# Four-layer attention and feed-forward kernel on one core: attention scores in float32 row bands, output bias on GpSimd, layer 3's correlation loops in 64x64 tiles

## The chip, the core and the metric

The kernel is one program on one core of a Trainium2 chip. The metric is device time in microseconds of that core, lower is better. Engines: PE (TensorE, matmuls; its weight loads are listed as PEld), DVE (VectorE), ACT (ScalarE), POOL (GpSimd) and SP (SyncE, which here only issues DMAs). Each engine works through its own list in order and waits on semaphores that others raise.

## The reference

`x` is 2 batches x 1024 rows x 256 features; `ctx` has 154 rows per batch. Four layers follow each other, each `x = x + attention(layernorm(x), ctx)` and then `x = x + ffn(layernorm(x))`. In layers 0 to 2 the attention has 16 heads of 16 features:

```python
q, k, v = split(x_n @ Wq + bq), split(ctx @ Wk + bk), split(ctx @ Wv + bv)
# layer 2 has no biases, and turns q and k by rotary angles
out = softmax(q @ k.T / 4) @ v
x = x + out.reshape(...) @ Wo + bo
```

Layer 3's attention is an autocorrelation: a circular correlation of q and k over 1024 positions, its mean over a head's features, the 6 best shifts and their softmax, the sum of v rolled by these shifts with these weights, and an output projection. The feed-forward parts: layer 0 squares a ReLU between two ternary weight matrices with a low-rank addition; layer 1 adds a dense gated part and, for each row, 32 rows of an expert table chosen by top-8 in 4 heads; layer 2 has 8 experts (2 chosen) and 2 shared ones; layer 3 has 8 experts (2 chosen). All is float32.

## The kernel before

**Chunks and order.** `x` stays in SBUF as `x_sb`, 16 tiles of 128 rows; a chunk `c` is 4 tiles (512 rows). The attention of a chunk of layers 0 to 2 is called here (layer, c). The twelve run in the order `A_ORDER`: (0,0) (0,1) (1,0) (1,1) (0,2) (0,3) (1,2) (1,3) (2,0) (2,1) (2,2) (2,3). `plan()` writes down every item of these layers with an assumed duration and what it waits for, ranks items by the longest path behind them, and from that fixes once, ahead of the run, the order of the list of every engine. Attention uses PSUM banks 0 to 3, the normalised rows, projections and keys banks 4 and 5, the feed-forward parts banks 6 and 7. Layer 3 is a fixed sequence whose phases begin with `enter` and end with `leave`: a phase starts when the other engines have ended theirs.

**Scores before.** Float32 values are split in three bfloat16 parts. Queries: PE projects (L686), ACT writes a float32 and a bfloat16 copy (L1099, L1100; in layer 2 DVE applies the rotary turn, L1337 to L1341), DVE subtracts and rounds to the other parts (`split`, L1325 to L1327), SP writes the parts to DRAM (L1779) and reads them back in 7 DMAs (L1788) so that the 7 pairs of parts of one head stand in 112 partitions. The keys go the same way (L1801, L1811). There is one buffer of queries, so the read of a chunk waits for the last score of the chunk before.

**One attention chunk.** The first pass (`p1`): 12 units, each of 6 (or 4) heads of one row tile, PE L726, then DVE takes the maximum over the 154 keys (L1385; L1388 and L1389 for the units of 4). PE turns the maxima (L734), ACT copies them (L1114), a DMA puts them as row 112 beside the queries (L1794). The second pass (`s`): for each head one bfloat16 matmul of 113x128x512 (L744) in banks 0 and 1 by turns and one exponential on ACT (L1121); for each group of four heads the last 26 keys (L752, L1128); then the weighting with v (`w`): L763 over the rest keys of four heads, and four matmuls of 32 columns each (L766), one per head, each with its own moving operand and its own 32 partitions of bank 3; ACT copies (L1132). Then transposes and division (L776, L1397, L1398, L783), and the output projection, where a one-row matmul adds the bias in layers 0 and 1 (L793, L796), and DVE adds to `x_sb` (L1322).

**The expert rows of layer 1.** For each row tile 32 table rows are fetched in 8 groups of 4. GpSimd issues 4 indirect DMAs per group (L1691) into a ring of 4 groups; DVE multiplies (L1261), ACT sums (L1048), DVE and ACT weigh (L1268, L1269, L1057), DVE adds three rows (L1278 to L1280), GpSimd the fourth (L1702, L1705). A group's slot is free when these adds are done.

**Layer 3.** `corr(b)`: per batch `b` and half `g` of the features, for two blocks `N` of 512 positions 10 accumulating matmuls of 128x128x512 (L969). Their stationary operand `kst` holds 8 heads' keys as diagonal blocks of 16x16, all else is zero. ACT copies the result to `c1` (L1219, L1220), SP writes it to DRAM (L1842) and reads it skewed (L1847), `top(b)` sums over features on PE (L958), and picks shifts and weights on DVE (L1575 to L1592); SP writes the weights to DRAM (L1830) and reads them shifted for every row (L1834). `out3(b)` is the second loop of the same size (L981, stationary `vst`, also diagonal blocks), ACT copies (L1228), the output projection (L992) and the add to `x_sb`. The sequence on PE is corr(0), projection of chunks 2 and 3, top(0), corr(1), first half of out3(0), top(1), second half, projection, the layer norm of chunk 0, out3(1). On DVE top(1) stands ahead of the adds of out3(0).

Of the kernel before, what the change touches and what calls it, by code (L numbers as in the profile page):

```python
# [10 lines left out]
P = 128  # L11
B, T, D = 2, 1024, 256
S = 154
# [5 lines left out]
SP_ = 160  # L19
# [17 lines left out]
Q_PARTS, K_PARTS = (0, 0, 0, 1, 1, 1, 2), (0, 1, 2, 0, 1, 2, 0)  # L37
NB = len(Q_PARTS)
MROW = NB * DH
SWAP = [lane ^ 1 for lane in range(32)]  # L40
MAX_UNITS = [(i, h, min(h + 6, H)) for i in range(TI) for h in range(0, H, 6)]
# [7 lines left out]
FFN3_PACK = dict(gate=KT * E3, we=KT * E3 * D, be=D)  # L49
CONST_PACK = dict(ident=P, mask8=8, padrow=1, iota8=8, selh=2 * 32, valid=SP_)  # L50
# [22 lines left out]
def plan():  # L73
# [26 lines left out]
    def kv(layer, b):  # L100
        item = (layer, b)
        shared.append(("kv",) + item)
        old = (layer - 1, 2 * b + 1) if layer else None
        k1 = add("PE", ("kv",) + item, 5.0, ld["kv", layer], ("SP", ("in", "ctx")), ("SP", ("in", "const")), banks[0])
        k2 = add("ACT", ("kv",) + item, 0.9, k1, parts[0])
        k3 = add("DVE", ("kv",) + item, 8.0 if layer == 2 else 5.5, k2, old and ("PE", ("w",) + old + (G4 - 1,)),
                 ld["rope", 0 if b == 0 else 2] if layer == 2 else None)
        banks[0] = k3
        parts[0] = add("SP", ("kvW",) + item, 0.1, k3, land=4.0)
        return add("SP", ("kvR",) + item, 0.7, parts[0], old and ("PE", ("r",) + old + (G4 - 1,)), land=5.0)  # L110
# [23 lines left out]
    def queries(layer, c, xt, k):  # L134
        item = (layer, c)
        shared.append(("Q",) + item)
        q1 = add("PE", ("Q",) + item, 3.3, xt, ld["q", PIECE_AT[k]])
        use["xta"] = q1
        if layer < 2:
            q2 = add("ACT", ("Q",) + item, 2.8, q1, parts[0], use["xa"])  # L140
            q3 = add("DVE", ("Q",) + item, 3.2, q2)
            banks[0] = q2
        else:
            q3 = add("DVE", ("Q",) + item, 9.0, q1, parts[0], use["xa"], ld["rope", c])
            banks[0] = q3
        use["xa"] = q3
        before = A_ORDER[k - 1] if k else None
        parts[0] = add("SP", ("QW",) + item, 0.1, q3, before and ("SP", ("L",) + before), land=3.8)
        return add("SP", ("L",) + item, 0.7, parts[0], before and ("PE", ("r",) + before + (G4 - 1,)), land=10.0)

    def attention(layer, c, k, keys_in, queries_in):
# [7 lines left out]
        for u in range(NU):  # L159
            p = pe("p1", 0.65, *((on("PE", "p1", u - 1), u > 1 and on("DVE", "p1", u - 2)) if u else  # L160
                                 (queries_in, keys_in, before and ("DVE", ("y",) + before + (TI - 1,)))), n=(u,))
            top = add("DVE", ("p1", layer, c, u), 1.15, p)
        p = pe("mt", 0.6, top)
        a = add("ACT", ("mt", layer, c), 0.6, p)
        last = add("SP", ("mt", layer, c), 0.1, a, land=2.3)
        for G in range(G4):
            for j in range(4):
                h = 4 * G + j
                z = (G, j - 2) if j >= 2 else (G - 1, j + 2)
                last = pe("s", 0.38, last, z[0] >= 0 and on("ACT", "s", *z), n=(G, j))  # L170
                add("ACT", ("s", layer, c, G, j), 0.62, last, h >= 6 and on("PE", "w", (h - 6) // 4),
                    on("ACT", "s", G, j - 1) if j else G and on("ACT", "r", G - 1))
            last = pe("r", 0.6, last, G and on("ACT", "r", G - 1), n=(G,))
            a = add("ACT", ("r", layer, c, G), 0.72, last, on("ACT", "s", G, 3), G >= 2 and on("PE", "w", G - 2))
            w = pe("w", 2.2, a, G and on("ACT", "w", G - 1), n=(G,))
            add("ACT", ("w", layer, c, G), 0.62, w)
        for G in range(G4):
# [1786 lines left out]
```

## Time and profile before

| | us |
|---|---|
| median of 3 runs | 2049.45 (2047.57 to 2050.88) |
| the profiled execution | 2054.53 |
| its span | 2052.7 |
| busy: PE / DVE / ACT / POOL | 1449.3 / 1186.3 / 805.8 / 659.3 |

The span is the time from the first to the last instruction of the profiled execution. Matmuls are pipelined, so a busy PE is not PE at its peak. The granted clock of PE over the span was 0.816 of full speed. Busy shares are means over stages that differ: the gathers of expert rows run from 395 to 1429 us only.

### The profile page before, as it was taken

Reading aid. Unit: us, or ns where it says so; the run is one execution under the profiler, and the core shown is the slowest. Engines: PE = TensorE matmul, PEld = TensorE weight load, DVE = VectorE, ACT = ScalarE, POOL = GpSimd, SP = SyncE. Lnnn points to the kernel's source line nnn. Section 1 sums busy time; section 2 is a strip of 40 time slices with the busy share of each in tenths; the row PEclk is TensorE's granted clock in tenths of the full one; section 3 lists DMA queues with packets and bytes.
Section 4 is the critical chain, followed back from the end, with each engine's and each line's share of the span. In section 5 each row is a group of like instructions: output and inputs, shape, how many; then the busy total and the mean of one; then the engine's idle time right before and its main releaser. Section 6 shows DMA issues by size and latency. Waiting matters only on the chain.

```text
span 2052.7 us, 17985 instructions
## 1 busy us (share of the span) xinstructions
PE 1449.3 (71%) x5190; PEld 752.3 (37%) x5190; DVE 1186.3 (58%) x3091; ACT 805.8 (39%) x2135; POOL 659.3 (32%) x672
## 2 busy tenths in 40 slices
PE   4788686876864865544365467567788668998998
PEld 2344343432432433222223333333444334344444
DVE  7342426588765856877578677776533223331665
ACT  2334143456563665344363548437343012101210
POOL 0000000235576676757565576674000000011000
PEclk7799798877775876766678688778899999999999
DMA  8331431537459567555655756853300011210000
GB/s 230 63 37 16 59 47 26 86 94 163 125 160 211 146 194 176 151 139 166 154 146 163 161 159 174 191 157 99 57 1 8 0 43 25 57 53 15 11 11 21
DMA packets 106513, 205.04 MB, mean 100 GB/s; under 512 B 32624, under 2 KB 68080, under 8 KB 105776
## 3 DMA queue, kind: packets, MB, share of 16 engines
q0 software_dynamic: 40960, 134.25, 24.2%
q1 hardware_dynamic: 65456, 69.66, 16.5%
q8 instruction: 41, 0.67, 0.1%
q14 instruction: 56, 0.46, 0.1%
HBM read 187.94 MB, written 15.73 MB: 99 GB/s over the span
## 4 chain that ended last, share of the span: by engine, by line
PE 40%; DVE 18%; POOL 13%; DMA 11%; issue 9%; ACT 7%; SPq 1%; ACTq 0%; DVEq 0%; POOLq 0%
POOL bufR L1691 11%; DMA bufB<-scr_queries 6%; PE psum L1012 6%; PE psum L905 5%; DMA bufR<-in_table,rowid 4%; PE psum L981 3%; PE psum L969 3%; PE psum L915 2%; DVE m L1385 2%; POOL half_sum L1705 2%; PE psum L835 2%; PE psum L871 2%; PE psum L843 1%; PE psum L793 1%; PE psum L726 1%
## 5 line engine op out<-in xcount | busy, mean ns | idle before, releaser
L1691 POOL DMA_INDIRECT bufR<-in_table,rowid x512 | 542.6, 1060 | 647.7 <-DVE prob L1498 391.2
L1048 ACT ACTIVATE bufR<-bufR 128x256 f32<-128x256 f32 x512 | 205.6, 406 | 222.3 <-DVE bufR L1261 213.2
L1261 DVE TENSOR_TENSOR bufR<-bufR 128x1024 f32<-128x1024 f32 x128 | 161.4, 1261 | 146.9 <-DMA bufR<-in_table,rowid 146.3
L905 PE MATMUL psum<-xtf,wf 128*128 128x512 f32 x320 | 165.1, 664 | 45.7 <-DVE x_sb L1545 34.2
L726 PE MATMUL psum<-bufB 112*128 112x154 bf16 x768 | 92.8, 276 | 142.4 <-DMA bufB<-scr_queries 77.2
L1713 POOL TENSOR_TENSOR x_sb<-x_sb,wattn 128x256 f32<-128x256 f32 x16 | 11.0, 722 | 418.3 <-ACTq L509 376.9
L1385 DVE TENSOR_REDUCE m<-psum 128x6 f32<-128x924 f32 x96 | 105.8, 1116 | 66.1 <-PE psum L726 63.2
L726 PEld LDWEIGHTS psum<-bufB 112*128 112x128 bf16 x768 | 70.1, 118 | 189.4 <-issue 104.5
L744 PE MATMUL psum<-bufB 113*128 113x512 bf16 x192 | 76.1, 432 | 79.5 <-ACT bufR L1121 62.2
L1322 DVE TENSOR_TENSOR x_sb<-x_sb,psum 128x256 f32<-128x256 f32 x128 | 50.8, 417 | 139.3 <-PE psum L992 50.0
L915 PE MATMUL psum<-wf,bufR 128*128 128x256 f32 x320 | 93.8, 447 | 50.9 <-DVE bufR L1536 42.5
L1121 ACT ACTIVATE bufR<-psum 128x512 f32<-128x512 f32 x192 | 109.4, 596 | 45.3 <-PE psum L744 45.1
L1705 POOL TENSOR_TENSOR half_sum<-half_sum,bufR 128x256 f32<-128x256 f32 x112 | 92.4, 825 | 105.6 <-ACT bufR L1057 102.7
L1012 PE MATMUL psum<-wf,xtf 128*128 128x512 f32 x256 | 121.1, 632 | 0.5 <-DVE x_sb L1655 0.5
L905 PEld LDWEIGHTS psum<-xtf,wf 128*128 128x128 f32 x320 | 64.9, 212 | 129.2 <-issue 71.6
L871 PE MATMUL psum<-xtf,wf 128*128 128x512 f32 x128 | 80.4, 786 | 36.9 <-DVE bufR L1456 36.9
L1048 ACT ACTIVATION_READ_ACCUMULATOR bufR<-bufR 128x1 f32 x512 | 97.3, 190 | 0.0
L915 PEld LDWEIGHTS psum<-wf,bufR 128*128 128x128 f32 x320 | 67.9, 221 | 76.9 <-issue 66.5
L1057 ACT ACTIVATE bufR<-bufR,ew 128x256 f32<-128x256 f32 x128 | 63.8, 500 | 62.6 <-DVE ew L1269 61.3
L763 PE MATMUL psum<-bufR,bufB 128*128 128x512 f32 x96 | 66.8, 784 | 27.5 <-ACT bufR L1128 26.2
L1545 DVE SCALAR_TENSOR_TENSOR x_sb<-psum,bufR,x_sb 128x256 f32<-128x256 f32 x128 | 53.1, 478 | 52.0 <-PE psum L915 51.5
L1536 DVE TENSOR_TENSOR bufR<-bufR,psum 128x512 f32<-128x512 f32 x40 | 27.4, 685 | 96.3 <-ACT bufR L1176 96.0
(236 smaller groups left out, 2693.6 us busy)
## 6 DMA issues: line engine op xcount, KB each, us to landing
bufB<-scr_queries SPq DMA_DIRECT2D x84, 256.0 KB
scr_queries<-bufB SPq DMA_DIRECT2D x12, 768.0 KB
bufR<-in_table,rowid POOLq DMA_INDIRECT x512
wf<-in_ffn SPq DMA_DIRECT2D x2, 2304.0 KB, 14.5
bufB<-scr_keys SPq DMA_DIRECT2D x42, 80.0 KB
bufR<-in_ffn SPq DMA_DIRECT2D x1, 2696.5 KB, 16.3
wattn<-in_attn SPq DMA_DIRECT2D x4, 641.0 KB
bufR<-scr_roll SPq DMA_DIRECT2D x4, 592.0 KB
```

The costliest lines, as they stand in the source:

```text
L726: ins = mm(psum[:, pair + z, at:at + S], queries[0:MROW, h, i * P:(i + 1) * P], keys(b)[0:MROW, h, 0:S], start=True, stop=True)
L744: mm(bank(j % 2), keys(b)[0:MROW + 1, 4 * G + j, 0:P], queries[0:MROW + 1, 4 * G + j, :], start=True, stop=True).then_inc(at_s2, 1)
L871: ins = mm(bank(6 + r), w1(name)[:, kt, m * P:(m + 1) * P], xtf[:, kt, :], start=kt == 0, stop=kt == KT - 1)
L905: ins = mm(bank(6 + r), gu[:, kt, r, :], xtf[:, kt, :], start=kt == 0, stop=kt == KT - 1)
L915: ins = mm(psum[:, 6 + i // 2, i % 2 * D:(i % 2 + 1) * D], hm2[:, GUS.index(m) % 7, i * P:(i + 1) * P], down2[:, m, :], start=m == ms[0], ...
L1012: ins = mm(bank(y % 4), xtf[:, kt, i * P:(i + 1) * P], w3("we")[:, kt, e * 512:(e + 1) * 512], start=kt == 0, stop=kt == KT - 1)
L1048: own.mark(act(row, row, ACT.Identity, accum_out=dots[:, g % 4, j:j + 1]))
L1121: act(probs[h % 6], bank(j % 2), ACT.Exp).then_inc(at_ex, 1)
L1261: tt(rows, rows, cast(xg[c % 3][:, i, :].unsqueeze(1), [P, GRP, D]), ALU.mult).then_inc(f1_mu, 1)
L1385: eng.reduce_max(m4[:, i, h0:h1].rearrange("p (a b) -> p a b", a=2), psum[:, pair:pair + 2, 0:3 * S].rearrange("p a (b s) -> p a b s", b=3 ...
L1691: eng.indirect_dma_start(ring[:, s * GRP + j, :], None, io["table"], bass.IndirectOffsetOnAxis(ap=rowid[c % 3][:, at + j:at + j + 1], axis ...
L1705: eng.tensor_tensor(half_sum[:, :], half_sum[:, :], up, ALU.add).then_inc(f1_half, 1)
```

## The change

- **Scores.** Queries and keys stay float32 in SBUF, nothing is split or goes through DRAM, and the maxima stay in SBUF. A band of 32 partitions holds two heads; `keysm[..., par, :]` is the keys with the other head of each pair set to zero. A first-pass unit is two float32 matmuls of 32x128x308 in two bands (four heads), 16 units per chunk. A second-pass burst is four float32 matmuls of 32x128x512, one per band, into banks 0 to 3, and four bfloat16 matmuls with a constant `sel` that subtract the maxima; then ACT takes two exponentials of 1024 columns. A burst starts when ACT has done with the one before. Per chunk there are 4 such bursts and 2 for the rest keys. There are two buffers of queries.
- **Keys and values.** The rest keys of v come from one full matmul with a repeated context `ctx4`; the v bias is added by DVE.
- **Output bias.** GpSimd adds it to `x_sb` (4 adds per chunk, layers 0 and 1), after the chunk's layer norm has read it; its list is shared with the gathers.
- **Layer 3.** Both loops run as 64x64 tiles, with the blocks that are zero left out: per `u` four matmuls of 64x64x512. The results lie in another layout, so 6 DMAs write each `c1`, and ACT copies in `out3(b)` come after each half. `Wo` comes with layer 3's feed-forward weights.
- `plan()` has new durations and no DMA items of the scores; all lists come out in a new order.

```diff
-Q_PARTS, K_PARTS = (0, 0, 0, 1, 1, 1, 2), (0, 1, 2, 0, 1, 2, 0)
+BANDS, PAR = 4, 2
-MAX_UNITS = [(i, h, min(h + 6, H)) for i in range(TI) for h in range(0, H, 6)]
+MAX_UNITS = [(i, g, half) for i in range(TI) for g in range(2) for half in range(2)]
...
             def first_pass(layer, c, u):
-                for h in range(h0, h1):
-                    z, at = (h - h0) // 3, (h - h0) % 3 * S
-                    ins = mm(psum[:, pair + z, at:at + S], queries[0:MROW, h, i * P:(i + 1) * P], keys(b)[0:MROW, h, 0:S],
+                for z in range(2):
+                    r = band(2 * side + z)
+                    ins = mm(psum[:, 2 * (u % 2) + z, 0:PAR * S], q[r, g, i * P:(i + 1) * P], keysm[r, g, b, :, 0:S],
                              start=True, stop=True)
...
-            def score(layer, c, G, j):
+            def score(layer, c, g, par):
...
+                elif par:
+                    eng.wait_ge(at_ex, 12 * k + 6 * g + 2)
+                else:
+                    eng.wait_ge(at_ex, 12 * k + 6)
+                    eng.wait_ge(at_ou, 4 * k + 2)
+                for z in range(BANDS):
+                    mm(bank(z), keysm[band(z), g, b, par, 0:P], q[band(z), g, :], start=True, stop=False)
+                for z in range(BANDS):
+                    ins = mm(bank(z), sel[band(z), 2 * g + par, :], mt[band(z), :], start=False, stop=True)
+                ins.then_inc(at_s2, 1)
...
             def corr(b):
                 for g in range(2):
-                    for N in range(2):
-                        for u in range(U):
-                            ins = mm(bank(2 * g + N), kst(b, g)[:, u, :], qx[:, g, 16 * u + N * 512:16 * u + N * 512 + 512],
-                                     start=u == 0, stop=u == U - 1)
+                    for u in range(U):
+                        for N in range(2):
+                            for r in range(2):
+                                h = half(r)
+                                ins = mm(psum[half(N), 2 * g + r, :], kst(b, g)[h, u, h], qx[h, g, 16 * u + N * 512:16 * u + N * 512 + 512],
+                                         start=u == 0, stop=u == U - 1, skip_group_check=True)
                     ins.then_inc(co_c, 1)
...
             def project_out(layer, c, i):
-                if layer < 2:
-                    ins = mm(psum[:, at, 0:D], valid[:, 0:P], wattn[0:1, AC["bo"]], start=False, stop=True)
...
+                for side in range(2):
+                    act(probs[side][:, par:4:2, :], psum[:, 2 * side:2 * side + 2, :], ACT.Exp).then_inc(at_ex, 1)
...
-                split(qf, [qparts[:, z] for z in range(3)]).then_inc(sk_p, 1)
...
+                for par in range(PAR):
+                    ts(keysm[:, :, b, par, :], kts, parity[:, par:par + 1], None, ALU.mult)
+                    ins = ts(keyr[:, :, b, 32 * par:32 * par + 32], kts[:, :, P:SP_], parity[:, par:par + 1], None, ALU.mult)
...
+            def add_bias(layer, c):
+                eng.wait_ge(ld_o, 16 * (PIECE_AT[chunk(layer, c)] + 1))
+                eng.wait_ge(fr_xn, TI * (front_of["a", layer, c] + 1))
+                for i in range(TI):
+                    ins = eng.tensor_tensor(x_sb[:, c * TI + i, :], x_sb[:, c * TI + i, :], wattn[:, AC["bo"]], ALU.add)
+                ins.then_inc(at_bo, 1)
...
-            def load_queries(layer, c):
-                for z in range(NB):
-                    eng.dma_start(queries[z * DH:(z + 1) * DH], scrq[Q_PARTS[z]].rearrange("(h d) n -> d h n", d=DH))\
-                        .then_inc(sk_rd, 16)
-            def turn_max(layer, c):
-                eng.dma_start(queries[MROW:MROW + 1], mt[:, :]).then_inc(at_mr, 16)
...
-                    eng.dma_start(scr1[a], c1[g]).then_inc(co_wr, 16)
+                    for r in range(2):
+                        for N in range(2):
+                            eng.dma_start(scr1[a, half(r), N * 512:(N + 1) * 512], c1[g][half(N), r * 512:(r + 1) * 512])\
+                                .then_inc(co_wr, 16)
+                        eng.dma_start(scr1[a, half(r), T:T + 16], c1[g][half(0), r * 512:r * 512 + 16]).then_inc(co_wr, 16)
```

`out3(b)` changes as `corr(b)` does, with `vst` and `roll` in place of `kst` and `qx`.

## Rows read from the trace of the kernel before

**Rows 1.** The page, part 2: PE clock granted, in 40 slices.
```profile
PEclk7799798877775876766678688778899999999999
```
**Rows 2.** Windows by stage: length, busy per engine (instructions), PE clock, DMA share, GB/s.
```profile
0.00:395.00 395.00, 286.11 (x1284) 152.87 (x1284) 183.62 (x498) 138.58 (x240) 2.97 (x17) 0.83 0.36 66
395.00:1429.00 1034.00, 639.09 (x2320) 335.61 (x2324) 754.72 (x1911) 535.25 (x1678) 645.31 (x640) 0.74 0.61 157
1429.00:1687.00 258.00, 188.07 (x694) 102.89 (x687) 95.93 (x265) 76.91 (x113) 0.00 (x0) 0.93 0.09 16
1687.00:2052.00 365.00, 336.05 (x896) 160.90 (x896) 152.07 (x420) 55.03 (x104) 10.98 (x16) 0.95 0.11 33
```
**Rows 3.** Chain that ended last: shares by line, then pieces: start, us, what.
```profile
POOL bufR L1691 11%; DMA bufB<-scr_queries 6%; PE psum L1012 6%; PE psum L905 5%; DMA bufR<-in_table,rowid 4%; PE psum L981 3%; PE psum L969 3%; PE psum L915 2%; DVE m L1385 2%; POOL half_sum L1705 2%; PE psum L835 2%; PE psum L871 2%; PE psum L843 1%; PE psum L793 1%; PE psum L726 1%
...
107.96 15.41 DMA bufB<-scr_queries
...
1466.34 14.10 DMA bufB<-scr_queries
```
**Rows 4.** Waits from 395 to 1429: who <- whom: us, times, longest.
```profile
POOL bufR L1691 <- issue: 133.1, 398, 2.0
POOL half_sum L1705 <- ACT bufR L1057: 102.7, 21, 18.7
...
PE psum L726 <- DMA bufB<-scr_queries: 55.9, 5, 19.9
POOL bufR L1691 <- DVE x_sb L1280: 55.4, 25, 9.4
```
**Rows 5.** Groups of instructions: shapes, count | busy us, mean ns of one | idle before.
```profile
L1121 ACT ACTIVATE bufR<-psum 128x512 f32<-128x512 f32 x192 | 109.4, 596 | 45.3 <-PE psum L744 45.1
L1385 DVE TENSOR_REDUCE m<-psum 128x6 f32<-128x924 f32 x96 | 105.8, 1116 | 66.1 <-PE psum L726 63.2 <-issue 1.1
L796 PE MATMUL psum<-wattn,const 1*128 1x256 f32 x64 | 32.2, 595 | 0.0
L1388 DVE TENSOR_REDUCE m<-psum 128x3 f32<-128x462 f32 x48 | 30.3, 632 | 8.5 <-PE psum L726 7.8 <-issue 0.8
L1325 DVE TENSOR_TENSOR xa<-xa,bufB 128x1024 f32<-128x1024 f32 x12 | 15.3, 1271 | 26.2 <-ACT bufB L1100 26.0
L1713 POOL TENSOR_TENSOR x_sb<-x_sb,wattn 128x256 f32<-128x256 f32 x16 | 11.0, 722 | 418.3 <-ACTq L509 376.9 <-DVEq L509 41.4
L1219 ACT ACTIVATE bufR<-psum 128x1024 f32<-128x1024 f32 x4 | 4.1, 1023 | 60.3 <-PE psum L969 60.3
```
**Rows 6.** Timeline of PE, weighting and FFN 1: start, us, line, rows*columns, count.
```profile
91.48 2.05 PE L763 MATMUL psum<-bufR,bufB 128*128 128x512 f32 x2
93.46 1.94 PE L766 MATMUL psum<-bufR,bufB 128*32 128x512 f32 x8
...
342.07 1.13 PE L863 MATMUL psum<-wf,bufR 64*128 64x256 f32 x8 [2.33 <-DVE bufR L1461]
```
**Rows 7.** Timeline of layer 3's loops and the selection.
```profile
1713.95 34.60 PE L969 MATMUL psum<-bufR,bufB 128*128 128x512 f32 x80
...
1763.58 3.62 PE L958 MATMUL psum<-bufR,const 128*32 128x512 f32 x8 [1.46 <-ACTq L509]
...
1767.34 1.21 DVE L1575 COPY bufR<-psum 16x1024 f32<-16x1024 f32 x1 [16.34 <-PE psum L958]
...
1784.81 0.80 SPq L1830 DMA_DIRECT2D scr_roll<-bufR  x2
...
1843.20 1.23 SPq L1834 DMA_DIRECT2D bufR<-scr_roll  x2
...
1849.83 1.40 DVE L1304 BATCH_NORM_STATS2 stats<-x_sb 128x6 f32<-128x256 f32 x4
...
1858.79 35.12 PE L981 MATMUL psum<-bufR,bufB 128*128 128x512 f32 x80
```
**Rows 8.** Windows after the second read of the weights: columns as in Rows 2.
```profile
1853.00:1858.00 5.00, 0.94 (x5) 0.97 (x6) 1.66 (x3) 2.07 (x4) 2.39 (x4) 0.52 0.00 0
```

More of the change, by code:

```diff
@@ L136, in queries @@
         shared.append(("Q",) + item)
-        q1 = add("PE", ("Q",) + item, 3.3, xt, ld["q", PIECE_AT[k]])
+        q1 = add("PE", ("Q",) + item, 3.6, xt, ld["q", PIECE_AT[k]])
         use["xta"] = q1
+        old = k >= 2 and ("PE", ("r",) + A_ORDER[k - 2] + (1,))
         if layer < 2:
-            q2 = add("ACT", ("Q",) + item, 2.8, q1, parts[0], use["xa"])
-            q3 = add("DVE", ("Q",) + item, 3.2, q2)
-            banks[0] = q2
-        else:
[L144 to L149, printed above, removed]
+            banks[0] = add("ACT", ("Q",) + item, 1.3, q1, old)
+        else:
+            banks[0] = add("DVE", ("Q",) + item, 5.0, q1, old, ld["rope", c])
+        return banks[0]
     def attention(layer, c, k, keys_in, queries_in):
@@ L182, in attention @@
             a = add("ACT", ("o", layer, c, g), 0.62, p)
+        if layer < 2:
+            bias = add("POOL", ("bo", layer, c), 3.0, ("ACT", ("N4", "a", layer, c)), ld["o", PIECE_AT[k]])
+        else:
+            bias = None
         for i in range(TI):
-            p = pe("y", 1.2, a, ld["o", PIECE_AT[k]], i and on("PE", "y", i - 1), n=(i,))
-            out = add("DVE", ("y", layer, c, i), 0.43, p)
+            p = pe("y", 0.9, a, ld["o", PIECE_AT[k]], i and on("PE", "y", i - 1), n=(i,))
+            out = add("DVE", ("y", layer, c, i), 0.43, p, bias)
         return out
@@ L714, in first_pass @@
                 k, b = chunk(layer, c), c // 2
-                i, h0, h1 = MAX_UNITS[u]
-                pair = 2 * (u % 2)
+                i, g, side = MAX_UNITS[u]
+                q = queries[:, k % 2]
                 if u == 0:
@@ new lines, in score, with score_rest @@
+                for z in range(BANDS):
[3 more added lines that the diff above has]
+                ins.then_inc(at_s2, 1)
+            def score_rest(layer, c, g):
+                k, b = chunk(layer, c), c // 2
+                q = queries[:, k % 2]
+                eng.wait_ge(at_ex, 12 * k + 6 * g + 4)
+                for side in range(2):
+                    for z in range(2):
+                        r = band(2 * side + z)
+                        mm(psum[half(z), side, :], keyr[r, g, b, :], q[r, g, :], start=True, stop=False, skip_group_check=True)
+                for side in range(2):
+                    for z in range(2):
+                        r = band(2 * side + z)
+                        ins = mm(psum[half(z), side, :], selr[r, g, :], mt[r, :], start=False, stop=True, skip_group_check=True)
@@ L1363, in kv @@
                     own.wait()
-                    own.link(tt(kts, kts, ksw, ALU.add))
-                own.link(eng.tensor_copy(kparts[:, 0], kts))
-                split(kts, [kparts[:, z] for z in range(3)]).then_inc(kv_p, 1)
+                    own.link(tt(kts[:, :, 0:S], kts[:, :, 0:S], ksw[:, :, 0:S], ALU.add))
+                if layer:
+                    eng.wait_ge(at_s2, 6 * (chunk(layer - 1, 2 * b + 1) + 1))
+                for par in range(PAR):
+                    ts(keysm[:, :, b, par, :], kts, parity[:, par:par + 1], None, ALU.mult)
+                    ins = ts(keyr[:, :, b, 32 * par:32 * par + 32], kts[:, :, P:SP_], parity[:, par:par + 1], None, ALU.mult)
+                ins.then_inc(kv_p, 1)
                 eng.wait_ge(kv_v, j + 1)
```

377 lines of the change are left out of this document (166 added, 211 removed).

## The prediction

> **What bounds the kernel now.** I read the windows by stage first. They cut the span at the first gather (395 us) and after the last (1429), at the end of layer 2 (1687) and at the end [rows 2]. No engine is full in the first three: PE is busy for 72%, 62% and 73% of them, DVE for 73% of the second. Only in the last is PE 92% busy. So the first three are held by handoffs, and the chain of waits says by which. The gather instructions on GpSimd are 11% of it, the read of the split queries 6%, which is 121 us in seven pieces of about 14 to 20 us, the first at 107.96 and the last at 1466.34 [rows 3]. The other five chunks have their read beside other work. In the middle stage GpSimd is the closest to full: 645 us busy and 133 us in issue, 778 of 1034 [rows 2, 4]. Its other idle time is in waits for ACT (103) and DVE (55), that is, for ring slots not yet given back [rows 4]. Five times PE stands on the read of queries, 55.9 us in all [rows 4], and as every list is fixed, DVE and ACT then stand on PE. In layer 3 the two loops are the chain: 34.60 us per batch and loop [rows 7].
>
> **Do tiles of the array run side by side?** Everything that follows hangs on this, and the trace shows two of the three kinds. Four matmuls of 32 columns (8 pieces: a float32 matmul is two) take 1.94 us; one full matmul (2 pieces) takes 2.05 beside it [rows 6]. So four column tiles cost one. Four matmuls of 64 rows and 256 columns, 8 pieces, take 1.13 us [rows 6]; a piece of 512 takes 34.60/80 = 0.43 at the high clock [rows 7], so 8 pieces of 256 in a row would take 1.73, in pairs 0.86 plus the pipeline's end. So row tiles pair too. Bands of 32 rows and 64x64 tiles are in no row. Bounds: one matmul's time for a burst of four, or four. I take the first, as both neighbours do.
>
> The Trainium skill, "TensorE: Matmul & The Clock Gate", Part 3, gives 3.07x, not 4x, for four row tiles of K=32 and N=512. Estimated from that page, each of the 72 bursts would cost 0.3 of 0.86 to 1.7 us more, 19 to 37 us of PE, and the sum below would be about 1905. The column tiles above show no such loss. "TensorEngine Tiling (Array Packing)", Tiling Modes, speaks against the change as well: a change of mode drains the array. From L763's start to L766's are 1.98 us where two pieces at the low clock are 1.72 [rows 6, 7], which agrees with at most 0.26 per change; some 10 more changes a chunk would be 31 us of PE, beside waits for the most part.
>
> **Layer 3, from 1713.95.** Each loop of a batch is 20 groups of four tiles, 2 pieces each: 20 x 2 x 0.43 = 17.3 for 34.6, four times. What is late next is the selection between the loops. By rows, with corr(0) starting at 0:
> - corr(0) ends at 17.3 (before 34.6). To top(0) it was 15.0 (1748.55 to 1763.58) [rows 7], with copy, write and skewed read in it; twelve DMAs per batch in place of two, on SP ahead of the read, add 1: top(0) at 33.3, corr(1) at 36.9, its end at 54.2.
> - DVE's selection: copy at 1767.34, weights handed to SP at 1784.81, 17.5 [rows 7]. Then write and shifted read: the second read starts at 1843.20 [rows 7] and the DMA engines are idle from 1853 on [rows 8], so about 10, and 2.5 for the write before it. Ready at 36.9 + 17.5 + 12.5 = 67. So out3(0) starts at 67 and not at 55: PE stands for 12 us that corr(1) used to cover, and starts again at the low clock (+2).
> - Half of out3(0), 8.6, top(1) 3.6 [rows 7], half: 90. But top(1) ends at 81, DVE is in its selection until 98.5, and the adds of out3(0) stand behind it in DVE's list. PE does two of the four projections and waits. Adds done at 104. Before, they were done at 1849.83, that is 135.9.
> - Layer norm to out3(1) as before, 1849.83 to 1858.79: 113 (before 144.8). The second read is ready at 98.5 + 12.5 = 111, just hidden.
> - out3(1) saves 17.4, and loses 0.6 as both copies come after its end.
>
> Sum: 32 + 17 = 49 of the 69 that the loops lose; I take 48. Bounds: 38 (reads slower by 5 each, all low clock) and 55.
>
> **Start to the first gather, 395 us.** Out: three reads on the chain, about 15.6 each (the first is at 107.96 [rows 3]), 47 us. Also the head: the first unit of chunk (0,0) can follow the query projection and doesn't wait for DRAM; the ternary weights then compete for DVE, so I take 13 (bounds 0 and 30). In: the bursts. Before, exponentials (596 ns each [rows 5]) ran beside matmuls. Now a burst is 1.07 us of PE at the high clock or 2.1 at the low (2 pieces of float32, 1 bfloat16 pass taken as half a piece of 0.43), then ACT 2 x 1.02 [rows 5] with PE idle, four times, and twice a shorter one: some 17 to 24 us per chunk beside nothing of its own, where the 12.5 us of exponentials had the weighting (4 x 4.0 at the low clock [rows 6]) beside them. Alone that is 8 to 16 per chunk; feed-forward work fills part, I take 5: +20 for four chunks. First-pass: a unit on DVE of 616 columns lies between 632 (462) and 1116 ns (924) [rows 5], 0.79; 16 units are 12.7, as before (8 x 1.12 + 4 x 0.94). PE's side of a unit is 0.52 at the high clock but 1.03 at the low: +4 there, inside the 5. The one-row bias matmuls, 32 us of PE in eight chunks, go [rows 5]. Sum -47 - 13 + 20 = -40; bounds -75 and +10.
>
> **The gathers, 1034 us.** GpSimd's floor is 778 + 4 bias items of 4 x 0.72 [rows 5] = 790, so at most 244 can go. What goes for certain: DVE's split, three instructions like L1325 (1.27, the cast less) [rows 5], 3.4 us x 7 chunks = 24 out of a list that the ring waits for. Of PE's 55.9 on reads I count 36, as the ring covers the rest. The bias items put 12 us in GpSimd's list, half of it in time that it has: +6. Bursts hold ACT no longer than before (8 x 1.02 against 16 x 0.60). Sum -54. Bounds: 0, if the ring sets the pace by itself, and -150, if what is held is the attention chain, which loses reads in each of seven chunks.
>
> **After the gathers to layer 3, 258 us.** Out: the read of (2,3), 14.1 [rows 3], and its write. The bursts of (2,3) lie beside layer 2's experts, and layer 2's own loop of one matmul, ACT, DVE, matmul is not touched. I take 12 more for (2,2) being further on at the last gather: -30; bounds 0 and -65.
>
> **The sum.** 2054.5 - 40 - 54 - 30 - 48 = 1882.5 against the profiled execution, which is 0.25% above the median; forecast 1878.
>
> **Rivals.**
> - *The ring sets its own pace.* For it: 778 of 1034 us, and 398 short waits called issue [rows 4]; against: 158 us of waits for ACT and DVE. The middle gains nothing: 1932.
> - *The attention chain held the middle.* For it: chunks whose reads stand open on PE; against: DVE 73% busy. The middle gives 130 and not 54: 1802.
> - *Bursts starve PE (slower).* Place: ACT's list from 395 to 1429. A chunk has 10 handoffs between PE and ACT with nothing in flight; each may queue behind ACT's sums of a gather group, and PE falls to the low clock, which it has already for half of this stage (0.74 [rows 2]; dips in [rows 1]). Price: half of ACT's share of a burst in queueing, 1.0, and 1.0 for PE's share at the low clock in place of the high (2.1 and 1.07), is 2.0 on 12 x 10 handoffs, 240, of which 20 are in the forecast: 2098. It decides from 1.6 per handoff on (1878 - 20 + 192 = 2050). Against: fewer handoffs, filled by other items.
> - *Bands and 64x64 tiles run one after another (slower), so the change doesn't do what it says.* A group of four tiles takes 3.43 in place of 1.72 for two full matmuls, 80 groups, +137 in place of -48; each of 72 bursts 2.6 more, each first pass 16 x 0.52, +287: 1878 + 48 + 137 + 287 = 2350. Against: [rows 6].
>
> **Chances.** Forecast 0.52 (its own range 1840 to 1915), ring 0.22, attention chain 0.16, starving 0.06, serial 0.04. A measurement of this kernel can tell 0.2% (4 us) from no change. Faster 0.89, same 0.02, slower 0.09. The range 1790 to 1965 leaves out the two slower rivals and the far end of the chain rival.
>
> **What would show it.** L1788, L1779 and L1325 are gone, and no chunk's first unit waits for a DMA. The loops of layer 3 take 17 to 18 us per batch each, with an idle of 10 to 14 ahead of out3(0) that ends on a DMA, and DVE's adds of out3(0) wait for PE no more but stand behind the selection. The first gather is at about 355, gather groups take about 7.6 us (now 8.1), and the last tile's add is at about 1335. A burst's four float32 matmuls start together. Wrong would be: loops of over 25 us, a middle stage longer than 1034, or PE's clock under 0.65 in it.

## The result, and the profile after

The changed kernel takes 1916.15 us (median of 4, 1904.04 to 1918.98) against 2050.16 for the kernel before in the same runs (2047.57 to 2061.31): ratio 0.9325, 95% interval 0.9272 to 0.9379. On another chip it took 1922.93 (median of 5), ratio 0.9350 (0.9327 to 0.9373), and experiments are read against both. The forecast was 1878 in a range of 1790 to 1965: faster, as forecast, but 38 us short of it and 1 us outside the forecast's own range. The profiled executions span 2052.7 before and 1916.5 after, 136 less, and all stages gained.

The windows by stage of the changed kernel, cut at the same events as [rows 2] (first gather, last tile's add, end of layer 2). Columns: stretch, length, then busy PE, PEld, DVE, ACT, POOL with their instructions, PE clock, DMA share, GB/s.

```profile
0.00:381.10 381.10, 312.58 (x1338) 155.26 (x1338) 166.21 (x482) 129.47 (x197) 14.36 (x34) 0.81 0.08 29
381.10:1349.50 968.40, 649.56 (x2538) 326.18 (x2538) 738.66 (x1888) 538.32 (x1630) 656.96 (x656) 0.78 0.55 149
1349.50:1591.00 241.50, 185.84 (x703) 100.26 (x702) 90.04 (x258) 63.55 (x89) 0.00 (x0) 0.93 0.02 6
1591.00:1916.50 325.50, 273.91 (x1280) 127.52 (x1280) 151.13 (x420) 55.03 (x102) 10.96 (x16) 0.90 0.14 39
```

The granted clock of the same execution in 40 slices, from the page, to set beside [rows 1]:

```profile
PEclk7779798788688687677677688889899898988999
```

| stage | before | after | measured | predicted |
|---|---|---|---|---|
| to the first gather | 394.9 | 381.1 | -14 | -40 |
| gathers | 1034 | 968.4 | -66 | -54 |
| to layer 3 | 258 | 241.5 | -16 | -30 |
| layer 3 to the end | 365.7 | 325.5 | -40 | -48 |

The middle did better than forecast by 12, and the three others worse by 26, 14 and 8. That the total still came near is in part luck: the middle gave more than forecast, for reasons that the runs resolve only in part, and that covers some of the shortfall. The middle's clock rose from 0.74 to 0.78, and PE is busy for 67% of it, not 62%.

The chain of waits of the changed kernel, shares by line, which answers to [rows 3]:

```profile
POOL bufR L1690 14%; PE psum L1010 6%; DMA bufR<-in_table,rowid 5%; PE psum L897 4%; PE psum L709 4%; PE psum L863 2%; DVE bufB L1384 2%; POOL half_sum L1704 2%; PE psum L907 2%; PE psum L758 2%; PE psum L733 2%; PE psum L676 2%; PE psum L761 2%; PE psum L827 2%; ACT bufR L1120 2%
```

Its waits among the gathers, from 381 to 1349.5, which answer to [rows 4] (who, for whom: us, times, longest):

```profile
POOL bufR L1690 <- issue: 123.7, 385, 2.0
...
POOL half_sum L1704 <- ACT bufR L1055: 68.6, 20, 10.6
...
POOL bufR L1690 <- DVE x_sb L1277: 37.8, 27, 7.5
```

The read of queries is gone from the chain. The gather instructions rose from 11% to 14%: 657 busy and 124 in issue are 781 of 968, as 778 of 1034 before. GpSimd's own work has hardly changed; its waits for ACT fell from 103 to 69 and for DVE from 55 to 38.

Three groups of the page, which answer to [rows 5]: the first pass on DVE, the exponentials on ACT, the bias on GpSimd (count | busy us, mean ns of one | idle before).

```profile
L1384 DVE TENSOR_REDUCE bufB<-psum 128x4 f32<-128x616 f32 x192 | 148.9, 795 | 64.7 <-PE psum L709 63.9
L1120 ACT ACTIVATE bufR<-psum 128x1024 f32<-128x1024 f32 x96 | 92.9, 1019 | 31.7 <-PE psum L735 31.5
L1710 POOL TENSOR_TENSOR x_sb<-x_sb,wattn 128x256 f32<-128x256 f32 x32 | 24.2, 790 | 265.9 <-DMA wattn<-in_attn 191.6
```

The first two durations are as forecast (0.79 and 1.02 us), the third is 0.79 for 0.72.

Bursts, from the timeline of the changed kernel: one as the clock is high, one of weightings beside it for the size of a full matmul.

```profile
143.94 1.14 PE L733 MATMUL psum<-bufB 32*128 32x512 f32 x8
144.90 0.39 PE L735 MATMUL psum<-bufB 32*128 32x512 bf16 x4
...
151.91 1.02 PE L758 MATMUL psum<-bufB 128*128 128x512 f32 x2
```

Four float32 matmuls of 32 rows (8 pieces) take 1.14 us, one full matmul (2 pieces) 1.02. Bands do run side by side. The four bfloat16 matmuls are listed with 0.39, but they start before the others end: all eight take 1.35 (143.94 to 145.29), so they add 0.21, half a piece, as forecast. The forecast had 1.07 for the eight; the 0.28 more is for the most part the end of the pipeline (a full matmul has 0.16 of it), which it left out.

Layer 3 in its timeline, which answers to [rows 7]: PE's loops and selections, then DVE's and SP's rows.

```profile
1618.81 17.40 PE L963 MATMUL psum<-bufR,bufB 64*64 64x512 f32 x160
...
1652.06 5.29 PE L950 MATMUL psum<-bufR,const 128*32 128x512 f32 x8 [2.33 <-DMA bufR<-scr_corr]
1657.28 17.40 PE L963 MATMUL psum<-bufR,bufB 64*64 64x512 f32 x160
1689.39 10.72 PE L977 MATMUL psum<-bufR,bufB 64*64 64x512 f32 x80 [14.71 <-DMA bufR<-scr_roll]
1701.38 3.62 PE L950 MATMUL psum<-bufR,const 128*32 128x512 f32 x8 [1.26 <-DMA bufR<-scr_corr]
1704.93 8.81 PE L977 MATMUL psum<-bufR,bufB 64*64 64x512 f32 x80
...
1738.08 18.86 PE L977 MATMUL psum<-bufR,bufB 64*64 64x512 f32 x160
...
1657.49 1.21 DVE L1571 COPY bufR<-psum 16x1024 f32<-16x1024 f32 x1 [18.88 <-PE psum L950]
...
1674.97 0.78 SPq L1799 DMA_DIRECT2D scr_roll<-bufR  x2
1692.10 1.30 SPq L1820 DMA_DIRECT2D bufR<-scr_corr  x2
...
1721.85 1.41 DVE L1319 TENSOR_TENSOR x_sb<-x_sb,psum 128x256 f32<-128x256 f32 x4 [0.21 <-DVE bufR L1588]
```

160 pieces in 17.40 us are 40 steps of 0.435: four 64x64 tiles at the price of one. PE stands 14.71 us ahead of the first output loop for the shifted read, and DVE's adds come right behind its selection (L1588), both as forecast (an idle of 10 to 14 there).

### The profile page after: what moved, and what is told of

Read it like the earlier page. It is cut to its first block, busy times and chain, and to the rows that moved or that the text cites. A ratio compares the mean times of both kernels' runs of the same rounds, so it can differ in the third digit from the quotient of the medians.

```text
span 1916.5 us, 19104 instructions
## 1 busy us (share of the span) xinstructions
PE 1421.9 (74%) x5858; PEld 709.2 (37%) x5858; DVE 1146.0 (60%) x3047; ACT 786.4 (41%) x2017; POOL 682.3 (36%) x705
## 4 chain that ended last, share of the span: by engine, by line
PE 42%; DVE 17%; POOL 16%; issue 11%; ACT 7%; DMA 6%; SPq 1%; ACTq 0%; DVEq 0%; POOLq 0%
POOL bufR L1690 14%; PE psum L1010 6%; DMA bufR<-in_table,rowid 5%; PE psum L897 4%; PE psum L709 4%; PE psum L863 2%; DVE bufB L1384 2%; POOL half_sum L1704 2%; PE psum L907 2%; PE psum L758 2%; PE psum L733 2%; PE psum L676 2%; PE psum L761 2%; PE psum L827 2%; ACT bufR L1120 2%
## 5 line engine op out<-in xcount | busy, mean ns | idle before, releaser
L709 PE MATMUL psum<-bufB 32*128 32x308 f32 x768 | 158.7, 635 | 108.4 <-DVE bufB L1384 67.0
L1258 DVE TENSOR_TENSOR bufR<-bufR 128x1024 f32<-128x1024 f32 x128 | 157.3, 1229 | 132.1 <-DMA bufR<-in_table,rowid 132.1
L1384 DVE TENSOR_REDUCE bufB<-psum 128x4 f32<-128x616 f32 x192 | 148.9, 795 | 64.7 <-PE psum L709 63.9
L1719 POOL TENSOR_TENSOR x_sb<-x_sb,wattn 128x256 f32<-128x256 f32 x16 | 11.0, 722 | 374.6 <-ACTq L511 326.9
L709 PEld LDWEIGHTS psum<-bufB 32*128 32x128 f32 x768 | 65.2, 245 | 194.7 <-DVE bufB L1384 129.5
L1710 POOL TENSOR_TENSOR x_sb<-x_sb,wattn 128x256 f32<-128x256 f32 x32 | 24.2, 790 | 265.9 <-DMA wattn<-in_attn 191.6
L1319 DVE TENSOR_TENSOR x_sb<-x_sb,psum 128x256 f32<-128x256 f32 x128 | 49.3, 415 | 108.5 <-PE psum L835 34.6
L1120 ACT ACTIVATE bufR<-psum 128x1024 f32<-128x1024 f32 x96 | 92.9, 1019 | 31.7 <-PE psum L735 31.5
L733 PE MATMUL psum<-bufB 32*128 32x512 f32 x384 | 66.3, 764 | 42.5 <-ACT bufR L1120 24.8
L758 PE MATMUL psum<-bufB 128*128 128x512 f32 x96 | 64.8, 762 | 38.7 <-ACT bufB L1126 38.7
L1652 DVE SCALAR_TENSOR_TENSOR x_sb<-psum,bufR,x_sb 128x256 f32<-128x256 f32 x128 | 61.7, 483 | 35.8 <-PE psum L1010 31.9
```

What stands on the lines that cost most here:

```text
L709: ins = mm(psum[:, 2 * (u % 2) + z, 0:PAR * S], q[r, g, i * P:(i + 1) * P], keysm[r, g, b, :, 0:S], start=True, stop=True)
L733: mm(bank(z), keysm[band(z), g, b, par, 0:P], q[band(z), g, :], start=True, stop=False)
L1120: act(probs[side][:, par:4:2, :], psum[:, 2 * side:2 * side + 2, :], ACT.Exp).then_inc(at_ex, 1)
L1258: tt(rows, rows, cast(xg[c % 3][:, i, :].unsqueeze(1), [P, GRP, D]), ALU.mult).then_inc(f1_mu, 1)
L1384: eng.reduce_max(m4[:, i, :].rearrange("p (z r) -> p z r", z=BANDS)[:, 2 * side:2 * side + 2, PAR * g:PAR * g + PAR], psum[:, at:at + 2, 0 ...
```

## The experiments

Twelve runs. "Changed" stands for the changed kernel; stage lengths are of the profiled execution of each. Ratios are to the kernel before; against changed, 0.9325 and 0.9350 stand for it. Wherever an edit changes what the planner counts, all lists come out in another order too, so a run's difference holds the edit and the order; what order alone can do is shown further down.

**Layer 3 alone.** In the kernel before, only layer 3's two loops, its writes and its output projection.

```
-for N: for u: mm(bank(2g+N), kst[:, u, :], qx[:, g, ...])
+for u: for N: for r: mm(psum[half(N), 2g+r], kst[h, u, h], qx[h, g, ...])
```

> The kernel before with only layer 3's part of the change: both loops in 64x64 tiles, the twelve writes per batch, the output projection from halves. Theory 1 (the trace of the changed kernel): from the first loop of layer 3 to the end it is 41 us shorter than before (338.8 to 297.7), and nothing ahead of it reaches in, so 2050 - 41 = 2009, within 4. Theory 2 (my prediction): 48 us, so 2002. Rival: part of the 41 comes from the state in which the changed first stages leave the chip (clock, loads already there): under 35 us, over 2015.

Measured: 2009.82, ratio 0.9781 (0.9708 to 0.9855), 43 us under the 2053.25 that the kernel before took on the same chip. Its last stage:

```profile
1680.00:2007.70 327.70, 274.84 (x1280) 127.67 (x1280) 151.25 (x420) 54.34 (x100) 10.97 (x16) 0.90 0.14 39
```

327.7 for 365.7 is 38 of that in layer 3. The stages ahead of it, which the edit doesn't touch, were 7 us shorter in this execution, which is the noise of one profile. Theory 1 holds: layer 3 gives 38 to 40 by itself (from the start of the first loop to the end 38, of the 41 in changed), not 48, and hardly hangs on the rest of the change. The interval of the total also takes in 2002; the stage's own length decides.

**The round trip of the queries put back.**

```
+SP: write queries -> DRAM; 3 reads DRAM -> spare, each waits for the one before
 first_pass, u == 0: + wait for the last read
+plan(): these four items with their times
```

One thing is not as it was: in the kernel before, the reads of a chunk wait for the last score of the chunk before; here they start as soon as the queries are made.

> The changed kernel, but each chunk's queries go through DRAM again before the first unit of the first pass may start: one write and three reads in a row, each waiting for the one before, some 15 to 19 us; what is read is not used, and the order of the work is planned anew with these times. Theory 1 (the wait on the reads was on the path where PE stood for it, 30 us at the start, about 36 among the gathers, 14 after them): some 60 to 80 us slower, about 1985. Theory 2 (the ring of gathers keeps its own pace): only start and tail, 35 to 45 us, about 1955. Theory 3 (the attention chain holds everything, twelve times in a row): over 130 us, over 2045.

**DVE's split put back.**

```
+DVE, each chunk: spare = q - q; cast spare; spare = q - spare; then sk_p
+plan(): 3.2 us more; rank["DVE", ("tern", 2)] += 1000.0
```

The last part puts one item of layer 0's ternary weights ahead of all else on DVE.

> The changed kernel, but VectorE makes the three parts of the queries again for each chunk (two subtractions and a cast, 3.2 us, into a place that nobody reads), and the first pass waits for the last. Theory 1 (VectorE's list is what the ring waits for in the gathers): 7 x 3.2 = 22 us there and about 3.2 for each of 4 chunks outside: 30 to 38 us slower, about 1950. Theory 2 (VectorE has room in the gathers): only 12 to 16 us, about 1930.

**The output bias back on TensorE.**

```
 project_out: + mm(psum[:, at, 0:D], valid[:, 0:P], wattn[0:1, bo], stop=True)
-GpSimd: add_bias(layer, c), 8 items of 4 adds
 plan(): no bias items, 1.2 us for 0.9 per projection
```

> The changed kernel with the output bias back on TensorE, as a one-row matmul behind each of the four projections of a chunk, and none of the eight bias items on GpSimd. Theory 1: the chain of each chunk is 2.4 us longer at its end, 3 chunks of which count before the first gather (+7), and the 12 us that GpSimd no longer works give back 6 at most: 0 to 8 slower, about 1920. Rival (GpSimd's list bounds the gathers): 6 to 12 faster, about 1907. Rival (order alone): over 10 either way, with the difference spread over all stages.

Measured, in this order: 1974.31 (ratio 0.9614, 0.9561 to 0.9668), 1966.84 (0.9575, 0.9515 to 0.9636), 1940.16 (0.9438, 0.9387 to 0.9489). Against the two times of changed they cost 51 to 58, 44 to 51 and 17 to 24. Where, by the windows of the first three stages, columns as above: the round trip,

```profile
0.00:409.10 409.10, 317.60 (x1338) 156.82 (x1338) 167.49 (x482) 133.17 (x199) 14.35 (x34) 0.80 0.15 53
409.10:1394.80 985.70, 655.12 (x2538) 326.92 (x2538) 740.40 (x1888) 537.53 (x1628) 652.66 (x656) 0.78 0.56 159
1394.80:1643.00 248.20, 185.84 (x703) 99.51 (x702) 90.25 (x259) 63.36 (x89) 0.00 (x0) 0.93 0.04 14
```

the split,

```profile
0.00:397.60 397.60, 310.05 (x1338) 155.57 (x1338) 179.63 (x497) 130.88 (x197) 14.37 (x33) 0.80 0.08 28
397.60:1387.70 990.10, 660.31 (x2524) 329.86 (x2524) 752.69 (x1906) 536.92 (x1626) 662.68 (x656) 0.76 0.52 145
1387.70:1635.00 247.30, 187.35 (x718) 98.88 (x716) 93.91 (x262) 68.10 (x95) 0.00 (x0) 0.94 0.02 5
```

and the bias.

```profile
0.00:394.20 394.20, 324.41 (x1362) 158.11 (x1362) 164.31 (x482) 129.50 (x197) 3.34 (x18) 0.81 0.08 28
394.20:1380.20 986.00, 684.96 (x2572) 342.69 (x2573) 735.33 (x1887) 542.20 (x1632) 643.66 (x640) 0.76 0.52 146
1380.20:1622.00 241.80, 185.71 (x709) 98.66 (x707) 90.71 (x260) 65.33 (x91) 0.00 (x0) 0.94 0.02 6
```

Among the gathers the round trip costs 17 us (985.7 for 968.4), the split 22 and the bias 18. Each is about what an order alone moved in this stage (17 and 26, see below), so one by one these three are not resolved; the totals of the first two are.

The round trip's total lies between theory 1 (60 to 80) and theory 2 (35 to 45). It is less than a copy of the old reads. Among the gathers PE stands on it for

```profile
PE psum L719 <- DMA bufB<-scr_trip: 17.1, 2, 9.4
```

where it stood 55.9 us in 5 waits before [rows 4]. Theory 3 (the attention chain holds everything) would be over 130 in all and falls for reads of this kind.

The split costs 44 to 51 where theory 1 had 30 to 38. 16 of it come ahead of the first gather, and all of them in the first attention chunk (its projection ends at 125.3, in changed at 108.5), where DVE has the item that was put ahead from 35.6 to 47.7, in front of the first pass; in changed this work comes behind the first pass. Without these 12 us the split would be at 32 to 39, near theory 1.

For the bias, theory 1 (0 to 8) and the rival of GpSimd's list (6 to 12 faster) both fell: GpSimd works 13 us less among the gathers (643.66 for 656.96) and gains nothing. PE works 35 us more there, but the one-row matmuls are not half of it:

```profile
L791 PE MATMUL psum<-wattn,const 1*128 1x256 f32 x40 | 16.0, 483 | 0.0
```

The rest is the same work taking longer, at a clock of 0.76 for 0.78. The rival of order alone asked for over 10 us spread over all stages; there are 13, 18 and 0. So that the bias costs PE this much is not shown apart from order.

**Layer 1's first feed-forward chunk ahead in the planner.**

```
+for n in todo: if n is q1, sm1, gu1, tk1 or ix1 of chunk 0: rank[n] += 1000.0
```

> The changed kernel, but the planner always takes the items of layer 1's first feed-forward chunk (its queries, similarities, gates and the choice of rows) ahead of all others that are ready. In the changed kernel they take 98.5 us from the third output projection to the first gather (282.6 to 381.1), before 85.8 (309.1 to 394.9). Theory 1 (this chunk's chain stands behind the bursts and the first pass of the next attention chunk, by order alone): the first gather is 10 to 15 us earlier, the fourth attention chunk as much later, and the total 5 to 12 us shorter, about 1907. Rival (the ring's later pace takes it up, or the attention chain is the one that counts): first gather earlier, total within 3 us of 1916 or longer.

Measured: 1900.67, ratio 0.9267 (0.9212 to 0.9322): by the ratios 12 to 17 us less than changed. The waits between the third output projection and the first gather, in changed:

```profile
DVE bufR L1457 <- ACT bufR L1162: 27.1, 3, 10.8
```

and in this one:

```profile
DVE bufR L1460 <- ACT bufR L1165: 13.2, 2, 8.8
```

In changed, DVE stands 27.1 us for this chunk's gates, which wait on PE and ACT behind the next attention chunk's bursts; taken ahead it is 13.2. The first gather comes at 368.3 (381.1), and the gathers take 960.6 (968.4). Theory 1 holds for the first gather and for the total. One part of it fell: the fourth attention chunk was to be as much later, but its projection ends at 376.3, in changed at 391.9. So both chains gained by the new order.

**Bands that can't run side by side.**

```
-keysm[band(z), ...], q[band(z), ...]    (first pass, bursts, rest)
+keysm[band(0), ...], q[band(0), ...]
```

> The changed kernel, but all four bands of a first pass and of a burst read their rows from band 0, so that their matmuls need the same rows of the array. It leaves out three quarters of the scores (the output is of band 0 alone); the instructions are as many and of the same shapes. My prediction's serial case: each burst 2.6 us longer, each first pass 16 x 0.52, in all 287 us on the path: 2200. Rival (PE has room while it waits for ACT and DVE): a half of it, about 2060. If bands don't run side by side at all, nothing: 1916.

Measured: 2275.04, ratio 1.1103. A burst of it, as the clock is high:

```profile
107.14 3.67 PE L733 MATMUL psum<-bufB 32*128 32x512 f32 x8 [0.81 <-ACT bufR L1130]
110.65 1.02 PE L735 MATMUL psum<-bufB 32*128 32x512 bf16 x4
```

3.67 in place of 1.14, and with the bfloat16 matmuls 4.53 in place of 1.35: 3.2 more for a burst, where I had 2.6. The total is 355 over the mean of changed, not 287, and neither the 2200 nor the rival's 2060 held. PE is busy 485 us longer (1907.3 for 1421.9), so some three quarters of its extra time land on the path; the price was too low, as it left out the bfloat16 matmuls and the clock (0.772 for 0.827). What bands side by side are worth is thus far more than the whole change gained; without them the kernel would be 11% slower than before.

**A burst as two halves.**

```
-4 matmuls after both exponentials; 2 exponentials after them
+side 0: 2 matmuls after exponential 0; exponential 0 after them; side 1 likewise
```

> The changed kernel, but a burst of four heads is two of two heads: the second burst's first half may start after the first exponential, and the exponential of a half after that half. Theory 1 (handoffs between PE and ACT with nothing in flight were the bursts' price): 4 x 1.3 us less in each chunk that counts, some 6 before the first gather and 8 among and after them: 1902. Rival (PE's time counts: pairs take 1.3 us twice where four take 1.3 once, 48 x 1.3 = 62 us more of PE in all): 15 to 30 us slower, about 1938.

Measured: 1915.13, ratio 0.9340 (0.9298 to 0.9383): the same. PE is busy 36 us longer (1458.0 for 1421.9), less than the 62 I had, and the total doesn't move, so what the handoffs gained is perhaps about what pairs cost. Neither answer held, and the run doesn't tell the two sizes apart. The first gather was at 386.2.

**Only another order.**

```
-first = [... (f, 0.12) ...]
+first = [... (f, 0.3) ...]
```

> The changed kernel, but the planner counts 0.30 us instead of 0.12 from an item to what follows it on another engine; nothing else. It shows what an order is worth that is only different. Theory: within 10 us of 1916. Rival (the order was made to fit): over 15 us slower.

Measured: 1916.45, ratio 0.9346 (0.9305 to 0.9387): as expected. But stages moved: the first gather at 404.0, 23 later than in changed, and the gathers in 951.6, 17 shorter. So the first gather's time alone says little of the total, and a difference in one stage of some 20 us can be order. The next runs show that the total can move as much.

**Three more orders, with six writes for twelve.** All three have the first feed-forward chunk ahead, and this:

```
-for r: for N: dma(scr1[a, half(r), N*512:...], c1[g][half(N), r*512:...]); pad
+for N: dma(rows[:, :, N*512:...], mine[half(N)])    (both r in one); pad in one
```

> The changed kernel with layer 1's first feed-forward chunk ahead of all else in the planner, and six writes per batch of layer 3's correlations in place of twelve (both row halves in one transfer). Theory: the order is worth 16 us as measured (1900.7); the writes are issued 0.6 us apart, so six fewer take up to 3.6 us from the chain to each selection, of which the first is on the path: top(0) at 30 after the start of the first loop, not 33.3, and the second selection's read 3 earlier too: 295 from that start to the end, not 298: 1898. Rival (larger transfers land later by as much): 1901.

The second:

```
-q1, sm1, gu1, tk1, ix1 of chunk 0
+q1, sm1, gu1, tk1, ix1 of all four chunks
```

> As the kernel with the six writes, but all four feed-forward chunks of layer 1 are taken ahead. Theory (each quarter's row numbers come earlier, but the ring never waited for any but the first): no gain beyond the first, and the attention chain, which these chunks now delay, costs: 0 to 15 us slower than 1898. Rival: another 5 to 10 us faster, since the attention of layer 2 hangs on the gathers.

The third:

```
+for n in todo: if n is the norm, projection or attention of (2, 3): rank[n] += 1000.0
```

> As the kernel with the six writes, but the attention of (2,3) is also taken ahead of all else. In the changed kernel the last chunk of experts starts 11 us after the one before it ends, as it waits for the output projection of (2,3) (1475.7 to 1482.8), which ran beside those experts for 103.6 us. Theory (order there costs what the stage after the gathers fell short by): the last experts start right behind, 6 to 11 us faster than 1898: 1890. Rival (TensorE's work and handoffs fill that stage in any order): within 3 us of 1898.

Measured: 1900.01 (ratio 0.9281, 0.9226 to 0.9335), 1918.51 (0.9344) and 1917.93 (0.9352). Six writes give nothing. With twelve writes and the same order (the run with the first chunk ahead) SP issues the last write of the second batch at 1664.30 and the read that waits for it at 1670.50; with six, at 1660.46 and 1670.60. They are issued sooner and land later, so the rival of that run held.

All four chunks ahead lose the whole gain again, 18 us, more than the theory's 0 to 15. The loss is all among the gathers: 984.7 us, against 959.1 in the run with six writes, and the other stages are within 2. Which wait brings it is open. For the last order, its third stage:

```profile
1332.00:1590.00 258.00, 192.63 (x703) 101.81 (x702) 90.68 (x259) 62.10 (x88) 0.00 (x0) 0.92 0.02 5
```

The pause ahead of the last experts is shorter (4.6 us between the last large matmuls of one chunk and the first of the next, gate left out, where it was 11.6 in changed), but the stage takes 258.0 (241.7 in the run with six writes, 241.5 in changed), and the gathers take 966.8 (959.1). Neither answer held: the theory had 6 to 11 faster, the rival within 3 of 1898, and it is 18 slower than the run with six writes.

**Changed once more,** with no edit.

> The changed kernel itself once more, on the chip of another day's runs, since every experiment is read against its 1916 us. If the differences of 16 (the first feed-forward chunk taken ahead) and 24 (bias on TensorE) are of the kernels and not of the chip, its median is 1912 to 1920. Rival (the runs of one chip are a whole shorter): under 1908, and the gain of the order taken ahead falls to less than half.

Measured: 1922.93 (1921.18 to 1925.86), ratio 0.9350. It is 3 over the expected 1920, and far from the rival's 1908. By their ratios the two kernels with the first chunk ahead are 0.7 to 0.9% under this, and 0.5 to 0.6% under the first measurement of changed. That is 9 to 17 us. It is barely clear of noise: the interval of the first (to 0.9322) doesn't touch this one's (from 0.9327), the interval of the second (to 0.9335) does, and both touch that of the first measurement (from 0.9272).

## Why the prediction was right or wrong

The direction, the range and the main mechanism (bands side by side, loops of layer 3 at half length) were right. The terms of the sum were off, as follows.

**Start, "three reads on the chain, about 15.6 each, 47 us": the term that was most off.** A read on the chain of waits is not a read that the work waits for in full. Here is PE's timeline around the first two of them in the kernel before (L796 ends the output projection of one chunk, L726 is the first unit of the next; between the second pair PE does 5.7 us of other work):

```profile
119.35 0.69 PE L796 MATMUL psum<-wattn,const 1*128 1x256 f32 x2
123.51 1.31 PE L726 MATMUL psum<-bufB 112*128 112x154 bf16 x9 [3.46 <-DMA bufB<-scr_queries]
...
207.99 0.69 PE L796 MATMUL psum<-wattn,const 1*128 1x256 f32 x2
...
228.23 0.93 PE L726 MATMUL psum<-bufB 112*128 112x154 bf16 x6 [6.99 <-DMA bufB<-scr_queries]
```

and in the changed one (L788 and L709):

```profile
104.80 3.69 PE L788 MATMUL psum<-wattn,bufR 128*128 128x256 f32 x16 [0.78 <-ACT bufR L1134]
109.08 0.80 PE L709 MATMUL psum<-bufB 32*128 32x308 f32 x8 [0.58 <-DVE x_sb L1319]
```

The read from 107.96 to 123.4 [rows 3] lay beside the weighting and the projection of the chunk before, up to 120.0; only 3.5 us were beyond it. The second left 19.6. The third belongs to the fourth chunk, which the first gather doesn't need. After, 0.6 stays each time. So 22 us went, not 47, and that is 25 of the 26 us by which the stage fell short.
- The head: forecast -13, measured -11.5 (the first projection ends at 108.5, before at 120.0). The first unit starts 36 us earlier (29.7, before 66.0). From there to the end of the projection it is 79 us, before 54: this chunk now has the ternary weights and its own longer bursts in it.
- The bursts: forecast +20 over four chunks. Chunks two and three take 89.1 and 83.9 us from first unit to the end of their projection, before 85.2 and 81.5: +6.3. The other 13 are not in a chunk but in the feed-forward chunk that leads to the first gather (98.5 us, before 85.2; the recorded 85.8 starts at 309.1, where the projection's last matmul ends at 309.7). The run with that chunk ahead takes 12.8 of them back with the bursts as they are, so they are the order of the lists and not a price of bursts. That the two, 6.3 and 13.3, make up the forecast 20 is luck. In all -11.5 - 21.9 + 6.3 + 13.3 = -13.8.

**The gathers, -54 for -66.** Forecast were reads -36, split -24, bias +6. Put back, they cost 17, 22 and 18, which would be 57 of the 66. But each of these is about what an order alone moves here, and the 17 is for reads on which PE stands 17.1 us, not the 55.9 of [rows 4]. So it doesn't show that 36 was too much; a read that waits for the last score, as before, was not put back. Nor does it show a gain from the bias: of the 32.2 us of one-row matmuls [rows 5] 16 lie in this stage in the run that has them back. What is shown is the sum: the stage gained 66 where order alone moved 17 and 26.

**After the gathers, -30 for -16.** The reads and the split put back cost 7 and 6 here; I had 14 for the read. The 12 for (2,2) being further on didn't come. (2,2) is further on indeed: the experts that follow it start (with their gate) 39 us after the last add, before 60. But (2,3) then runs wholly beside them and takes 103.6 us, before 89.8, and the last experts wait for it. One order that was to mend this, (2,3) ahead, made the stage longer; others were not tried.

**Layer 3, -48 for -40.** Loops of 17.4, top(0) at 33.3, selection of 17.5 are as forecast. Mis-sized: top(0) at a granted clock of 0.67 in place of 1.00 (5.29 for 3.62), so corr(1) ends at 55.9 and not 54.2; write and shifted read 14.4 from SP's row to the loop, not 12.5; top(1) held at 82.6 by its skewed read, which SP issues behind its writes, where I had 77.4. The adds are done at 110 (104), out3(1) starts at 119.3 (113). From there to the end it is 15.5 shorter, forecast 16.8.

**Side by side.** The step on which all hung was right. The Trainium skill, "TensorE: Matmul & The Clock Gate", Part 3, gives 3.07x for four row tiles. Here the four float32 matmuls of a burst take 3.67 on one band and 1.14 on four, 3.2x with the pipeline's end in both, so the trace comes near the page. Most of the rest of the factor is that end, as a full matmul alone takes 1.02: from the start of the four to the start of what follows it is 3.51 and 0.96, 3.7x. The estimate from that page, 1905, is nearer to the result than mine, but not for its reason: the 0.12 us by which these four exceed a full matmul is 9 us over 72 bursts, not 19 to 37. What a change of tiling mode costs, the other rule that was weighed, no run here isolates.

**The rivals.** "The ring sets its own pace" fell with the middle's 66 us. "The attention chain held the middle" had 130 there and got 66, half of it. Starving didn't come: the middle's clock rose. "Serial" fell with the trace, and its price for the bursts and first passes was too low (355, not 287). Of the other signs, gather groups take 7.6 us, as forecast; the first gather (381) and the last tile's add (1349) came later than the 355 and 1335 that were named.

What stays open: how the middle's 66 us divide among reads, split, bias and order; what the second buffer of queries is worth, which no run took back; and why an order with a first gather 23 us later lost nothing in the end. A set of several orders for each edit would be needed to tell them apart.

## What to carry to other kernels

A transfer on the chain of waits is worth only what lies between the end of all work beside it and its landing; read that from the engine's rows on both sides before multiplying its length by its count. When every list is fixed by a planner, an edit also changes the order: here order alone moved one stage by 17 to 26 us and the total by 18, so a put-back run is worth reading only where its difference is larger, or where its own waits show what it did. And an experiment that puts a transfer back must also put back what the transfer waited for.

## What the runs showed of the hardware

- At the high clock four float32 matmuls of 32 rows in four bands take 1.14 us where the same four on one band take 3.67. 64x64 tiles in a long loop show no loss: 160 pieces take 17.40, 0.435 for each four, and 80 full pieces took 34.60, 0.43 each.
- Four bfloat16 matmuls of 512 columns behind them add 0.21 in four bands (0.39 with the pipeline's end) and take 1.02 on one band.
- Six writes in place of twelve, of the same bytes, left the read that waits for them where it was (the second batch's read is issued 73.8 us after the start of the first loop, with the same order of lists, in both).
